# A graph layer with edge gathers: two inverse roots per block go from ScalarE and VectorE to GpSimd, and the bias of the following layer goes into TensorE's sums

## The reference

```python
def _L1_gnn_ref(x, src, dst, ...):
    Wh = x @ W_w + W_b;  Uh = x @ U_w + U_b;  Vh = x @ V_w + V_b
    sigma = sigmoid((Wh * attn_l)[src] + (Wh * attn_r)[dst])
    h = Uh + segment_sum(Vh[src] * sigma, dst) / (segment_sum(sigma, dst) + 1e-06)
    mu = mean(h);  var = mean((h - mu) ** 2)
    h = (h - mu) / sqrt(var + 1e-06) * gamma + beta
    return x + relu(h)

def _L1_ffn_ref(x, W1, b1, Wg, bg, Wd, bd):
    H = gelu(xf @ W1 + b1, approximate=False)        # 1024 columns
    probs = softmax(H @ Wg + bg)                      # 8 experts, the largest is taken
    ...
x = x + _L1_gnn_ref(layernorm(x), ...)
x = x + _L1_ffn_ref(layernorm(x), ...)
```

## Time and profile before

| what | value |
|---|---|
| three timed runs | 3047.15, 3048.69, 3051.67 us |
| span of the profiled execution | 3050.2 us |
| mean granted TensorE clock, share of full | 0.907 |
| busy over the span: PE, DVE, ACT, POOL | 82%, 79%, 38%, 45% |
| first gather of `stage_strips` starts, last one starts | 1783.55 us, 2804.42 us |
| last store of the stage starts | 2866.33 us |

### The profile page before, as it was taken

How to read it: one execution, slowest core, us unless ns; L and a number is a source line. 1 busy time by engine, 2 the same in 40 slices (tenths; PEclk the granted TensorE clock), 3 DMA queues, 4 the chain that set the end, 5 groups by cost and what they waited for, 6 DMA issues and landing times. The chain is left out here.

```text
span 3050.2 us, 49528 instructions
## 1 busy us (share of the span) xinstructions
PE 2502.4 (82%) x17163; PEld 1226.6 (40%) x17164; DVE 2395.6 (79%) x5109; ACT 1169.5 (38%) x2265; POOL 1359.9 (45%) x1627
## 2 busy tenths in 40 slices
PE   6899869999986999985999756777666777667598
PEld 3555544333353333334666421333333333323365
DVE  6999979999968999979343757777777777777477
ACT  5666750000020000002222434666666666666421
POOL 2888850000000000000650777777777777776055
PEclk8999989999998999995999876888888888888799
DMA  3000010000032000003341577888888888887343
GB/s 123 10 10 10 10 38 15 15 15 15 5 42 40 15 26 18 5 19 107 92 124 43 189 239 240 247 258 259 248 256 259 255 259 256 252 258 241 133 148 106
DMA packets 235579, 373.47 MB, mean 122 GB/s; under 512 B 83273, under 2 KB 165390, under 8 KB 233513
## 3 DMA queue, kind: packets, MB, share of 16 engines
q0 software_dynamic: 75536, 238.14, 25.9%
q1 hardware_dynamic: 156569, 128.66, 14.2%
q10 hardware_dynamic: 3200, 3.21, 0.4%
HBM read 324.84 MB, written 50.04 MB: 123 GB/s over the span
## 5 line engine op out<-in xcount | busy, mean ns | idle before, releaser
L1161 PE MATMUL dense_p_o<-dense_W,feat 128*32 128x512 f32 x7200 | 789.7, 594 | 23.4 <-DVE dense_W L1093 23.4
L1093 DVE SCALAR_TENSOR_TENSOR dense_W<-layer_B,steep,cnt 128x512 f32<-128x512 f32 x1200 | 796.7, 744 | 3.2 <-DVE dense_W L1093 1.8
L2461 POOL DMA_INDIRECT Wd<-tab_d,ixq x544 | 520.7, 957 | 171.2 <-issue 167.5
L1161 PEld LDWEIGHTS dense_p_o<-dense_W,feat 128*32 128x32 f32 x7200 | 261.4, 110 | 520.9 <-issue 399.9
L1572 POOL MEMSET edst<- 128x782 int32 x1 | 0.8, 752 | 936.6 <-POOLq L1210 936.6
L2639 PE MATMUL strips_p_sg<-strips_sv,strips_oh 128*32 128x512 f32 x2000 | 317.7, 713 | 92.7 <-DVE strips_sv L2504 92.7
L2627 PE MATMUL strips_p_b<-strips_wrs,strips_ohT 96*128 96x256 bf16 x1000 | 176.5, 306 | 223.2 <-DVE strips_ohT L2475 204.6
L729 POOL TENSOR_SCALAR mix_L<-mix_back,encode_lowT 128x128 bf16<-128x128 f32 x520 | 320.5, 634 | 55.6 <-PE mix_p_c L889 54.8
L2568 ACT ACTIVATE strips_p_s<-strips_tv 128x1024 f32<-128x1024 f32 (+1 forms) x250 | 225.2, 901 | 163.9 <-DVE strips_sv L2504 149.7
L1117 ACT COPY dense_part<-dense_p_o 128x512 f32<-128x512 f32 x36 | 18.8, 594 | 645.5 <-PE dense_p_o L1161 645.5
L2461 POOL DMA_INDIRECT strips_G<-tab_d,ixq x240 | 229.7, 957 | 73.2 <-issue 71.3
(11 more groups left out here) (540 smaller groups left out, 3883.2 us busy)
## 6 DMA issues: line engine op xcount, KB each, us to landing
strips_row<-dlr_d SPq DMA_DIRECT2D x250, 96.0 KB
ew<-in_ew SPq DMA_DIRECT2D x16, 1024.0 KB, 5.4
layer_B<-rise_d SPq DMA_DIRECT2D x12, 1024.0 KB, 4.8
hx_d<-hrow SPq DMA_DIRECT2D x24, 512.0 KB, 2.8
Wd<-tab_d,ixq POOLq DMA_INDIRECT x544
Wd<-in_fWd SPq DMA_DIRECT2D x8, 1024.0 KB, 9.0
tab_d<-feat SPq DMA_DIRECT2D x50, 128.0 KB, 2.5
tab_d<-gated_in_rowg SPq DMA_DIRECT2D x25, 256.0 KB, 2.0
```

The costliest lines, as they stand in the source:

```text
L1093: o = nc.vector.scalar_tensor_tensor(out=out, in0=rise, scalar=C.steep[:, q * H + h:q * H + h + 1], in1=count, op0=ALU.max, op1=ALU.mult)
L1161: m = nc.tensor.matmul(p_o[c % 2][h * MT:(h + 1) * MT, a, 0:n], feat[:, q, h, lo:lo + MT], W[t % 3][:, h, 0:n], start=(q == 0), stop=(q == ...
L2461: gp.indirect_dma_start(out=G[n % RING][:, j, :], out_offset=None, in_=C.tab3[:, :], in_offset=bass.IndirectOffsetOnAxis(ap=index, axis=0) ...
```

## The change

In `stage_strips`, GpSimd now works out both inverse roots. A root is eight dependent instructions on 128 x 1 tiles (`newton`): one that adds epsilon and halves, one that makes a first guess by arithmetic on the bits as an integer, and three Newton steps of two instructions each; each waits for the one before through a semaphore. They are put among GpSimd's gathers by `inverse_root` and `roots_before`: when GpSimd has waited for the use of slot n - 12, it works out the roots that belong to groups ahead of that use, and then issues slot n. ScalarE's two Sqrt, VectorE's two reciprocals and its two additions of epsilon are gone; VectorE waits for the root one instruction later than before.

The bias of the 1024 columns is no longer a column operand of Gelu: three bf16 parts of it, prepared by GpSimd in `stage_experts` (`C.b1S`), are multiplied by a tile of ones and added to the sums, one bf16 product for each piece of 128 columns. So Gelu is one instruction of 1024 columns, at i = 18 (QC + 8) in place of 19. The DMA that loaded the bias as columns is gone, one that loads it as a row is in `stage_experts`. Some small tiles share memory.

```diff
@@ stage_experts, sync and gpsimd
+                sp.dma_start(b1r[:, :], A["fb1"].rearrange("(a f) -> a f", a=1)).then_inc(s_b1, 16)
...
+                nc.gpsimd.memset(C.b1S[:, :], 0.0).then_inc(s_b1s, 1)
+                gp.wait_ge(s_b1, 16)
+                gp.wait_ge(s_b1s, 1)
+                nc.gpsimd.tensor_copy(C.b1S[0:1, :], b1r[:, :]).then_inc(s_b1s, 1)
...
+                nc.gpsimd.tensor_copy(C.b1S[2 * QP:2 * QP + 1, :], b1r[:, :]).then_inc(s_b1s, 1)
@@ stage_strips, gpsimd
+                    def newton(root, var, eps, out, done):
+                        base = 7 * root
+                        nc.gpsimd.tensor_scalar(nw[:, :], var, eps, -0.5, ALU.add, ALU.mult).then_inc(s_nw, 1)
+                        gp.wait_ge(s_nw, base + 1)
+                        nc.gpsimd.tensor_scalar(ny[:, :].bitcast(I32), nw[:, :].bitcast(I32), -0.5, ROOT, ALU.mult, ALU.add).then_inc(s_nw, 1)
+                        gp.wait_ge(s_nw, base + 2)
+                        for n in range(3):
+                            nc.gpsimd.tensor_scalar(na[:, :], ny[:, :], ny[:, 0:1], nw[:, 0:1], ALU.mult, ALU.mult).then_inc(s_nw, 1)
+                            gp.wait_ge(s_nw, base + 3 + 2 * n)
+                            if n < 2:
+                                nc.gpsimd.tensor_scalar(ny[:, :], na[:, :], 1.5, ny[:, 0:1], ALU.add, ALU.mult).then_inc(s_nw, 1)
+                                gp.wait_ge(s_nw, base + 4 + 2 * n)
+                            else:
+                                nc.gpsimd.tensor_scalar(out, na[:, :], 1.5, ny[:, 0:1], ALU.add, ALU.mult).then_inc(done, 1)
+
+                    def inverse_root(step):
+                        b, i = divmod(step - QC, QC)
+                        if i == 1 and 0 <= b < NB:
+                            gp.wait_ge(s_var, b + 1)
+                            if b >= 1:
+                                gp.wait_ge(s_std2, b)
+                            newton(2 * b, mv[:, 1:2], 1e-6, rstd[:, :], s_std)
+                        if i == 3 and 0 <= b < NB:
+                            gp.wait_ge(s_var2, b + 1)
+                            gp.wait_ge(s_std, b + 1)
+                            newton(2 * b + 1, mv2[:, 1:2], 1e-5, rstd2[:, :], s_std2)
+
+                    rooted = [0]
+
+                    def roots_before(step):
+                        for n in range(rooted[0], step):
+                            inverse_root(n)
+                        rooted[0] = max(rooted[0], step)
+
                     for g in range(NG4):
                         b, i = divmod(g, QC)
                         n = slot(g)
                         if n >= RING and i <= QR:
                             gp.wait_ge(s_use, last_user(n - RING) + 1)
+                            roots_before(last_user(n - RING))
...
+                    roots_before((NB + 2) * QC)
@@ stage_strips, vector
-                            nc.vector.bn_aggr(mv[:, :], st[:, :]).then_inc(s_d, 1)
-                            v.wait_ge(s_d, 4 * b + 4)
-                            nc.vector.tensor_scalar(rstd[:, :], mv[:, 1:2], 1e-6, None, ALU.add).then_inc(s_var, 1)
+                            nc.vector.bn_aggr(mv[:, :], st[:, :]).then_inc(s_var, 1)
...
-                            v.wait_ge(s_std, b + 1)
-                            nc.vector.reciprocal(rstd[:, :], rstd[:, :]).then_inc(s_q, 1)
+                            v.wait_ge(s_var, b + 1)
                             nc.vector.scalar_tensor_tensor(out=h, in0=h, scalar=mv[:, 0:1], in1=gam[:, :], op0=ALU.subtract, op1=ALU.mult).then_inc(s_q, 1)
+                            v.wait_ge(s_std, b + 1)
@@ stage_strips, scalar
-                        if i == 2:
-                            act.wait_ge(s_var, b + 1)
-                            nc.scalar.activation(rstd[:, :], rstd[:, :], ACT.Sqrt).then_inc(s_std, 1)
-                        if i == QC + 2:
-                            act.wait_ge(s_var2, b + 1)
-                            nc.scalar.activation(rstd2[:, :], rstd2[:, :], ACT.Sqrt).then_inc(s_std2, 1)
...
-                        if i == QC + 9:
+                        if i == QC + 8:
...
-                            for q in range(FC):
-                                nc.scalar.activation(hidden(b)[:, q * P:q * P + P], ffn(b)[:, q * P:q * P + P], ACT.Gelu, bias=b1[:, q:q + 1]).then_inc(s_he, 1)
+                            nc.scalar.activation(hidden(b)[:, 0:F], ffn(b)[:, 0:F], ACT.Gelu).then_inc(s_he, 1)
@@ stage_strips, tensor
-                                    t = nc.tensor.matmul(ffn(b)[:, q * P:q * P + P], w1[:, kc, q * P:q * P + P], xT[:, kc * P:kc * P + P], start=(kc == 0), stop=(kc == KC - 1))
-                                t.then_inc(s_h, 1)
+                                    nc.tensor.matmul(ffn(b)[:, q * P:q * P + P], w1[:, kc, q * P:q * P + P], xT[:, kc * P:kc * P + P], start=(kc == 0), stop=False)
+                                nc.tensor.matmul(ffn(b)[:, q * P:q * P + P], C.b1S[:, q * P:q * P + P], onesb[:, :], start=False, stop=True).then_inc(s_h, 1)
```

More of the change, by code:

```diff
@@ L87 @@
 BIG = float(2.0 ** 100)
+ROOT = float(0x5F3759DF - 2 ** 22 - 2 ** 30)
 def skewed(eng, count, unroll, front, back, peel=0):
@@ L1822, in stage_experts @@
         b3 = sb("b3", [1, 3 * D]); b3m = sb("b3m", [1, 3 * D], BF16)
+        b1r = sb("b1r", [1, F]); b1m = sb("b1m", [1, F], BF16); s_b1 = sem("s_b1"); s_b1s = sem("s_b1s")
         def load_quarter(eng, q, s_ix):
@@ L1896, in _ @@
                 gp.wait_ge(s_bs, 7)
+                nc.gpsimd.memset(C.b1S[:, :], 0.0).then_inc(s_b1s, 1)
+                gp.wait_ge(s_b1, 16)
+                gp.wait_ge(s_b1s, 1)
+                nc.gpsimd.tensor_copy(C.b1S[0:1, :], b1r[:, :]).then_inc(s_b1s, 1)
+                gp.wait_ge(s_b1s, 2)
+                nc.gpsimd.tensor_tensor(b1r[:, :], b1r[:, :], C.b1S[0:1, :], ALU.subtract).then_inc(s_b1s, 1)
+                gp.wait_ge(s_b1s, 3)
+                nc.gpsimd.tensor_copy(b1m[:, :], b1r[:, :]).then_inc(s_b1s, 1)
+                nc.gpsimd.tensor_copy(C.b1S[QP:QP + 1, :], b1r[:, :]).then_inc(s_b1s, 1)
+                gp.wait_ge(s_b1s, 5)
+                nc.gpsimd.tensor_tensor(b1r[:, :], b1r[:, :], b1m[:, :], ALU.subtract).then_inc(s_b1s, 1)
+                gp.wait_ge(s_b1s, 6)
+                nc.gpsimd.tensor_copy(C.b1S[2 * QP:2 * QP + 1, :], b1r[:, :]).then_inc(s_b1s, 1)
+                gp.wait_ge(s_b1s, 7)
             @block.vector
@@ L2314, in stage_strips @@
         G = [C.Wd[:, k * FC * D:(k + 1) * FC * D].rearrange("p (h d) -> p h d", h=H) for k in range(NE)] + [sb(f"G{k}", [P, H, 2 * D]) for k in range(NE, RING)]
-        row = [sb(f"row{k}", [ST, H, P], BF16) for k in range(RR)]; ipt = sb("ipt", [ST, P]); ip = sb("ip", [ST, 1])
-        oh = [sb(f"oh{k}", [P, H, QP]) for k in range(4)]; nil = sb("nil", [P, 2 * D], BF16)
+        row = [sb(f"row{k}", [ST, H, P], BF16) for k in range(RR)]; ip = sb("ip", [ST, 1])
+        oh = [sb(f"oh{k}", [P, H, QP]) for k in range(4)]; nil = sb("nil", [ST, P], BF16)
         ohT = [sb(f"ohT{k}", [ST, H * P], BF16) for k in range(2)]
@@ L2383, in each_step @@
                          (last - 2, two + 2), (last - 2, two + 3), (last - 1, one + 4), (last - 2, two + 4), (last - 2, two + 5), (last, one + 2), (last, one + 3),
-                         (last - 1, one + 5), (last - 1, one + 6), (last - 1, one + 7), (last, one + 4), (last - 1, one + 9),
+                         (last - 1, one + 5), (last - 1, one + 6), (last - 1, one + 7), (last, one + 4), (last - 1, one + 8),
                          (last, one + 5), (last, one + 6), (last, one + 7),
-                         (last - 1, two), (last - 1, two + 1), (last, one + 9), (last - 1, two + 2), (last - 1, two + 3), (last - 1, two + 4),
+                         (last - 1, two), (last - 1, two + 1), (last, one + 8), (last - 1, two + 2), (last - 1, two + 3), (last - 1, two + 4),
                          (last, two), (last, two + 1), (last - 1, two + 5), (last, two + 2), (last, two + 3), (last, two + 4), (last, two + 5)):
@@ L2522, in tail @@
                         if i == 3:
                             if b == 0:
-                                v.wait_ge(s_w, 96)
+                                v.wait_ge(s_w, 80)
                                 v.wait_ge(s_wg, 2)
                                 nc.vector.tensor_copy(wgp[:, :, 0:NE], wgt[:, :, :]).then_inc(s_wg, 1)
+                            v.wait_ge(s_var, b + 1)
+                            nc.vector.scalar_tensor_tensor(out=h, in0=h, scalar=mv[:, 0:1], in1=gam[:, :], op0=ALU.subtract, op1=ALU.mult).then_inc(s_q, 1)
@@ L2527, in tail @@
                             v.wait_ge(s_std, b + 1)
-                            nc.vector.reciprocal(rstd[:, :], rstd[:, :]).then_inc(s_q, 1)
-                            nc.vector.scalar_tensor_tensor(out=h, in0=h, scalar=mv[:, 0:1], in1=gam[:, :], op0=ALU.subtract, op1=ALU.mult).then_inc(s_q, 1)
-                            v.wait_ge(s_q, 6 * b + 2)
```

(13 more changed lines are left out.)

33 lines of the change are left out of this document (14 added, 19 removed).

## The result

| | before | the change |
|---|---|---|
| median of 4 runs each (lowest to highest) | 3048.97 us (3047.15 to 3051.67) | 3220.34 us (3216.98 to 3231.19) |
| ratio, 95% interval | | 1.0567 (1.055 to 1.0584): 171 us slower |
| span of the profiled execution | 3050.2 us | 3215.3 us |
| first gather, last gather of the stage | 1783.55, 2804.42 | 1780.82, 2949.19 |
| last store of the stage | 2866.33 | 3030.50 |

A forecast was written before the change was run, and what follows sets the result against it. GpSimd's issuing of gathers was taken as the bound, 41.6 us a block. 45 roots x 2.5 = 113 us, plus 21 for the moved wait, plus 0, gave 134 us on the median: 3183 us, range 3130 to 3290.

The forecast's parts named there:

- The bound: In `stage_strips`, GpSimd issuing one gather after the other sets the pace: 1.262 us each, 41.6 us a block of 33.
- The price of a root: Among GpSimd's gathers: 8 x 0.33 - 0.13 = 2.5 us a root, 45 roots on the path, 113 us.
- c: Cost of one root instruction on GpSimd, from its start to the next one's: 0.33 us taken, ends 0.21 and 0.70.
- the 0.13 credited for the idle gap: Per root on GpSimd: arithmetic between two gathers replaces one 0.30 us idle gap, leaving 0.13 us less.
- The moved wait: VectorE's L2581 must wait for a root queued behind later gathers; free in steady state, 21 us paid once at the end.
- Nought, give or take 3: Work behind block 22's root: table loads and long Gelu go (4 us at most), two uncovered roots of 2.5 us each come.
- The Gelu part: In each block: shorter Gelu on ScalarE costed at nothing; eight bias products on TensorE hidden, 29 us in all without cover.
- Added in `stage_experts`: Seven more instructions on rows of 1024, hidden by POOL's 90.13 us of idle time; some 10 us without that cover.
- catch up: Rival: the chain bounds, POOL's gathers quicken behind roots, and fewer ScalarE table loads make it faster: 3008 us, 4 in 100.
- hide in the gaps: Rival: root instructions run in POOL's 0.30 us idle before each gather, leaving only the moved wait: 3070 us, 6 in 100.
- as dear as 128 columns: Rival: each root step on GpSimd takes what 128 columns take, counted from c = 0.58 on: 3318 us, 10 in 100.

## Why the prediction was right, and where it was off

*The bound.* A block of 33 gathers takes 41.6 us, and nothing on GpSimd is free: right, and shown. Unread instructions in its queue cost their full 3.05 us, while less gelu time on ScalarE (the place put back) gains nothing.

*The price of a root.* This is the term that was mis-sized: 2.5 us forecast, 3.05 to 3.07 measured (46 roots in 140.3 us when unread; in the change 147.5 us, of which some 6 are GpSimd's waits for a used slot). First to last gather was forecast at +113 us and came to +147.5: 46 x 0.57 is 26 of the 34.5 us between, a 46th root ahead of the last gather 2.5, and the 6 us of waits, which the sum did not have, the rest. Behind the last gather 19.4 came in place of 21, and 1.8 us less outside, so the spans differ by 165 where 134 was forecast. c came out at 0.38, from 2416.29 to 2419.33 in eight steps, where 0.33 was taken between 0.21 and 0.70: the five groups of short instructions take 105.6 us for 368, 0.29 in the mean and not 0.25, the gap is 0.10 and not 0.08, and a gather behind a root can last 0.28 longer, which more than eats the 0.13 credited for the idle gap. The measured time lies 37 us above the 3183, inside what the ends of c gave.

*The moved wait.* Forecast 21 us, "paid once, at the end": VectorE's L2581 of block 22 comes 21 us later against GpSimd's gathers, as said, and last gather to last store takes 81.3 us where "some 81" was forecast. That it is the place in the queue is shown by the two runs with earlier roots, where 31.6 and 33.9 us fewer are left behind the last gather (two roots went ahead with it, and the roots are dearer there, so 20 and 14 us of it show in the time), and by the unread roots, which do not have it. The close agreement is partly luck: from L2581 of block 22 to the last store are 92.2 us, 1.6 more than before, with the gelu's place in it. With the place put back they are 89.0, 1.6 less than before. "Nought, give or take 3" was two small things that nearly cancel, and the forecast knew only one of them.

*The Gelu part.* "Gelu, which may wait a little for them: hidden under the 41.6 us." In the change that was nearly right, since GpSimd had moved to 47.8 us a block; by itself it was wrong by 41 us. The prediction counted 40.2 us of chain against 41.6 and costed only what TensorE adds. It did not cost the move from i = 19 to 18: a wait of 2.2 to 2.7 us for TensorE, and two table loads and the gelu ahead of a pair of sigmoids that VectorE needs.

*Added in `stage_experts`.* Hidden as said: the new instructions end 80 us before the next gather has to start, against 90 before:

```profile
1602.47 1.03 POOL L1912 CAST b1S<-experts_b1r 1x1024 bf16<-1x1024 f32 x1
1683.67 1.04 POOL L2178 DMA_INDIRECT gated_in_yb<-ffn_out_d,back  x1 [80.17 <-remote]
```

*The rivals.* GpSimd did not catch up (the gathers stay 1.25 apart behind a root), so fewer table loads could not bring the time down: 3008 is out. The steps did not hide in the gaps: 3070 is out, by the unread roots. They were not as dear as 128 columns: c = 0.38, not from 0.58 on.

## What to carry to other kernels

Where two chains run side by side within a few per cent (41.6 and 40.2 us a block here), price an edit against each: one instruction in the queue of the first is paid in full, and the second can lose 41 us by an edit whose cost shrinks to 8 to 14 us as soon as the first gets slower. Taking work off an engine that does not bound buys nothing: the gelu got 1.16 us a block shorter, and the time stayed where it was (0.9999). For a small instruction moved to GpSimd, count its steps from start to start and what the next instruction loses, and put it where its input is ready, not where a buffer comes free, but look at what the other engines do beside it there.

## What was not expected of the hardware

The gather behind a root lasts 0.98 us in half of the cases and 1.23 in the other half in the change; where nobody reads the root and GpSimd waits for it itself, it is about 0.98 each time, after a gap, and a root costs the same. In the run with earlier roots GpSimd's short instructions became longer beside some instructions of VectorE; the longest in one block:

```profile
2438.94 0.93 POOL L2480 TENSOR_SCALAR strips_ny<-strips_na,strips_ny 128x1 f32<-128x1 f32 x1
```

VectorE's L2595 ran beside it from 2439.03, then L2578, which reads two tensors in SBUF, from 2439.35 to 2439.82; GpSimd's instruction ended at 2439.87. The Trainium skill (GPSIMD Engine Reference, "Specifications") says that GpSimd shares SBUF interfaces with VectorE and contends with its instructions of two SBUF inputs; L2578 is one. The row agrees in part: at its usual 0.26 us the instruction would have ended at 2439.20, before L2578 began, so L2595, with one tensor in SBUF, seems to have delayed it too. Counted over the stage of that run, from first to last gather: of the 384 short instructions, 155 ran with VectorE idle and 155 only beside such of its instructions as have an input in PSUM (its adds and multiplies, mostly); all of these have the shortest length of their line to within some 0.01 us. Of the 74 that met an instruction reading SBUF alone (L2595, L2578, the masks L2527 and L2530 mostly), 49 were longer by over 0.05, up to 0.68. In sum it is 17.5 us there and 5.4 in the change, where the roots meet mostly VectorE's waits, adds and multiplies.
